# Layer 0 of a gated cross-attention kernel: transposes of two heads' probabilities in two 64-row halves of the TensorE array, with another order of the side work

## What is computed

```
x  = x + tanh(g_xattn[0]) * L0_xattn(layernorm(x), ctx, ctx)      # 16 heads of 16
x  = x + tanh(g_ffn[0])   * L0_ffn(layernorm(x))                  # scan over the sequences
...
scores = einsum('bhqd,bhkd->bhqk', qh, kh) * scale
attn   = softmax(scores)                                          # 112 x 375 for a head
out    = einsum('bhqk,bhkd->bhqd', attn, vh)
c      = sigmoid(..) * c + sigmoid(..) * tanh(..)                 # step of the scan, three gates
```

## Time and profile before

| | |
|---|---|
| median of 3 runs | 2946.25 us (2937.28 to 2954.1) |
| span of the profiled execution | 2561.4 us |
| around the span, against the median | 384.9 us |
| TensorE busy | 2366.4 us, 92% |
| VectorE, ScalarE, GpSimd busy | 66%, 60%, 28% |
| layer 0, first score to last exponential | about 38 to 790 us of the span |

### The profile page before, as it was taken

The page is one execution under the profiler, slowest core; times in us unless marked ns, Lnnn a source line. Parts: engine busy times, 40 slices in busy tenths (PEclk is TensorE's granted clock), DMA queues, the critical chain, the costliest instruction groups (busy, mean ns, idle before and its releaser), DMA issues. The chain is left out here.

```text
span 2561.4 us, 63498 instructions
## 1 busy us (share of the span) xinstructions
PE 2366.4 (92%) x20058; PEld 1795.7 (70%) x20059; DVE 1692.1 (66%) x5327; ACT 1525.4 (60%) x4611; POOL 729.2 (28%) x863
## 2 busy tenths in 40 slices
PE   7999999999998999999999999999999869999950
PEld 5777777777776566666666666666666658888840
DVE  4776776777674567767667767766776645555559
ACT  3777777777773656656666666665665425545530
POOL 2000000000000023322322332332332347777740
PEclk8999999999999999999999999999999989999975
DMA  5111111111113211111111111111110366666659
GB/s 155 44 36 48 46 36 48 45 42 42 45 35 95 72 30 47 42 35 41 42 40 37 42 44 32 47 42 30 47 42 28 110 211 187 186 186 188 188 186 380
DMA packets 145288, 210.06 MB, mean 82 GB/s; under 512 B 23976, under 2 KB 108506, under 8 KB 145026
## 3 DMA queue, kind: packets, MB, share of 16 engines
q1 hardware_dynamic: 114322, 139.92, 18.7%
q0 software_dynamic: 26544, 60.21, 7.0%
q10 hardware_dynamic: 4160, 6.55, 0.7%
HBM read 118.21 MB, written 96.75 MB: 84 GB/s over the span
## 5 line engine op out<-in xcount | busy, mean ns | idle before, releaser
L1454 ACT ACTIVATE wup<-bank,nmax 112x375 f32<-112x375 f32 x512 | 297.3, 585 | 127.2 <-DVE nmax L1558 126.0
L766 ACT ACTIVATE prob<-bank,nmax 112x375 f32<-112x375 f32 x512 | 293.6, 586 | 55.7 <-DVE nmax L850 51.6
L850 DVE TENSOR_REDUCE nmax<-bank 112x1 f32<-112x375 f32 x512 | 255.4, 541 | 90.2 <-PE bank L588 90.2
L2045 POOL DMA_INDIRECT expert_results<-res,dest x288 | 280.2, 973 | 118.5 <-ACT res L2163 67.0
L1558 DVE TENSOR_REDUCE nmax<-bank 112x1 f32<-112x375 f32 x512 | 255.4, 541 | 36.0 <-PE bank L1250 36.0
L1895 POOL DMA_INDIRECT expert_rows<-rows,ids x248 | 237.2, 957 | 78.6 <-issue 69.0
L2163 ACT ACTIVATE res<-bank,xr 128x256 f32<-128x256 f32 x288 | 136.4, 474 | 190.7 <-PE bank L2077 189.6
L1868 POOL TENSOR_TENSOR stats<-stats,neg_half 112x1 f32<-112x1 f32 x64 | 35.7, 557 | 654.6 <-DVE stats L1589 652.2
L1313 PE MATMUL bank<-wup,wk 128*128 128x375 f32 x512 | 219.8, 512 | 2.1 <-DMA wup<-context_turned 0.9
L1019 POOL TENSOR_TENSOR stats<-stats,neg_half 112x1 f32<-112x1 f32 x64 | 35.1, 549 | 633.7 <-DVE stats L880 629.7
L1460 ACT COPY pT<-bank 128x336 f32<-128x336 f32 x512 | 201.1, 449 | 19.7 <-PE bank L1257 19.1
(11 more groups left out here) (255 smaller groups left out, 5001.6 us busy)
## 6 DMA issues: line engine op xcount, KB each, us to landing
xr<-expert_rows SPq DMA_DIRECT2D x288, 129.0 KB
wup<-expert_results SPq DMA_DIRECT2D x14, 1024.0 KB, 18.8
wdn<-expert_results SPq DMA_DIRECT2D x14, 1024.0 KB, 20.2
wdn<-in_L_ffn_W_down_dram SPq DMA_DIRECT2D x8, 1024.0 KB, 12.2
expert_rows<-nowhere SPq DMA_DIRECT2D x56, 129.0 KB, 3.1
x_and_h_in<-stage SPq DMA_DIRECT2D x32, 224.0 KB, 2.6
xt<-x_and_h_in SPq DMA_DIRECT2D x32, 224.0 KB, 2.8
context_turned<-ctxT SPq DMA_DIRECT2D x32, 187.5 KB, 2.3
```

The source lines that it names most:

```text
L766: nc.scalar.activation(prob[:, n % RING, :NK], s_bank[r][:NQ, :NK], ACT.Exp, bias=nmax[:, r:r + 1], accum_out=rsum[:, par, h:h + 1]).then_ ...
L850: nc.vector.tensor_reduce(nmax[:, r:r + 1], s_bank[r][:NQ, :NK], AX, ALU.max, negate=True).then_inc(maxed, 1)
L1454: nc.scalar.activation(prob[:, n % RING, :NK], s_bank[r][:NQ, :NK], ACT.Exp, bias=nmax[:, r:r + 1], accum_out=rsum[:, par, n:n + 1]).then_ ...
L2045: nc.gpsimd.indirect_dma_start(results_d, bass.IndirectOffsetOnAxis(ap=dest[:, n % DEST:n % DEST + 1], axis=0), res[:, n % RES, :], None, ...
```

## The change

Two heads are now turned together (`turn_pair`), three chunks each, every chunk as two transposes: probability rows 0 to 63 into bank `pt_bank[0]`, rows 64 to 111 into `pt_bank[1]`, each in its own rows of the array. ScalarE copies the first bank (2 x 3 x 64 = 384 columns) and VectorE the second (2 x 3 x 48 = 288) for every pair; each pair waits until both copies of the pair before are done. TensorE's order is uses n, pair n, scores, pair n+2, uses n+1 to n+3. ORDER_A has other slots, r1 goes to VectorE's lane, and the reciprocals move to slots 5 and 12 of `parts`. The cut diff shows the list, then TensorE's, ScalarE's and VectorE's parts in that order; ScalarE's `inverse` serves r0 alone, and `keep_pair` is on each of the two engines one copy of the 64 or 48 columns of all six chunks of a pair.

```diff
 ORDER_A = [
-    (0, "pre", "ctxT", "dve"), (1, "post", "va1", "dve"), (2, "pre", "k0", "act"), (2, "post", "wo", "dve"),
-    (4, "pre", "k1", "act"), (4, "pre", "xT", "dve"), (5, "pre", "q", "act"), (5, "post", "lnT", "dve"),
-    (6, "post", "h_in", "act"), (7, "pre", "v2", "dve"), (8, "post", "gate_f", "act"), (9, "own", "r0", "act"),
-    (11, "post", "gate_g", "act"), (12, "own", "va0", "dve"), (13, "own", "r1", "act"), (15, "pre", "v01", "dve"),
-    (15, "post", "gate_i", "act"),
+    (0, "pre", "ctxT", "dve"), (1, "post", "va1", "dve"), (1, "pre", "k0", "act"), (2, "post", "wo", "dve"),
+    (3, "pre", "k1", "act"), (5, "pre", "xT", "dve"), (6, "pre", "q", "act"), (6, "post", "lnT", "dve"),
+    (7, "own", "r0", "act"), (9, "own", "va0", "dve"), (9, "post", "h_in", "act"), (10, "pre", "v2", "dve"),
+    (11, "post", "gate_f", "act"), (13, "post", "gate_g", "act"), (14, "pre", "v01", "dve"),
+    (15, "post", "gate_i", "act"), (15, "own", "r1", "dve"),
 ]
...
-                def turn(i, n):
-                    wait_kept(pe, i, n - 1)
-                    pe.wait_ge(exped, H * i + n + 1)
-                    for c in range(KC):
-                        mm = pe.transpose(pt_bank[n % 2][:, c * NQ:(c + 1) * NQ],
-                                          prob[:, n % RING, c * P:(c + 1) * P], ident[:NQ, :NQ])
+                def turn_pair(i, n):
+
+                    wait_kept(pe, i, n)
+                    pe.wait_ge(exped, H * i + n + 2)
+                    for a in range(2):
+                        for c in range(KC):
+                            at = a * KC + c
+                            for half, rows_of in enumerate((slice(0, HALF_Q), slice(HALF_Q, NQ))):
+                                width = rows_of.stop - rows_of.start
+                                mm = pe.transpose(pt_bank[half][:, at * width:(at + 1) * width],
+                                                  prob[rows_of, (n + a) % RING, c * P:(c + 1) * P], ident[rows_of, rows_of])
                     mm.then_inc(turned, 1)
...
-                        turn(i, n)
-                        turn(i, n + 1)
                         uses.run(hooks, i, n, par, first, last)
+                        turn_pair(i, n)
                         next_scores(i, par, g, last)
+                        turn_pair(i, n + 2)
                         uses.run(hooks, i, n + 1, par, first, last)
-                        turn(i, n + 2)
-                        turn(i, n + 3)
...
-                        keep_turned(i, n)
                         uses.run(hooks, i, n, par, first, last)
-                        keep_turned(i, n + 1)
+                        keep_pair(i, n)
+                        keep_pair(i, n + 2)
+                        next_exponentials(i, par, n, last)
                         uses.run(hooks, i, n + 1, par, first, last)
-                        next_exponentials(i, par, n, last)
-                        keep_turned(i, n + 2)
                         next_exponentials(i, par, n + 1, last)
...
+                def keep_inverse(v):
+                    def f(p, par, n):
+                        misc = full(dve, "dve", n)
+                        nc.vector.tensor_copy(rT[:, v, :], misc[:, :NQ]).then_inc(lane_free["dve"], 1)
+                    return f
...
-                    if n == 8:
+                    if n == 5:
                         inverse(i, par, 0)
-                    if n == 10:
+                    if n == 12:
                         inverse(i, par, 1)
...
                         parts(i, n, par, first, last)
+                        keep_pair(i, n)
                         next_maximum(i, par, n, last)
                         next_maximum(i, par, n + 1, last)
+                        keep_pair(i, n + 2)
+                        next_maximum(i, par, n + 2, last)
+                        next_maximum(i, par, n + 3, last)
                         uses.run(hooks, i, n + 1, par, first, last)
                         parts(i, n + 1, par, first, last)
-                        keep_turned(i, n + 3)
-                        next_maximum(i, par, n + 2, last)
-                        next_maximum(i, par, n + 3, last)
```

More of the change, by code:

```diff
@@ L440, in layer0_phase @@
     PT_RING = 16
-    DVE_KEEPS = (3, )
+    HALF_Q = P // 2
     def head(n):
@@ L448, in loads, with pairs @@
         return (j - par) * 8 + 16
[L450 to L460, removed]
+    def pairs(i, n):
+        return (H * i + n) // 2
     def place(name):
@@ L514, in wait_kept @@
         def wait_kept(eng, i, n):
-            by_dve, by_act = kept(i, n)
-            wait(eng, kept_dve, by_dve)
-            wait(eng, kept_act, by_act)
+            wait(eng, kept_dve, pairs(i, n))
+            wait(eng, kept_act, pairs(i, n))
         def freed(eng, j, name):
@@ L752, in full, with pT_pair @@
                 return lane_bank[lane]
+            def pT_pair(n):
+                return pT[:, n % PT_RING:n % PT_RING + 2, :].rearrange("p a (c q) -> p (a c) q", c=KC)
             def room_in_pT(eng, i, n):
@@ L764, in exponentials, with keep_pair @@
                         wait(act, inverted, NV * (i - 1))
-                    wait(act, turned, H * i + n + 1 - RING)
+                    if H * i + n >= RING:
+                        act.wait_ge(turned, pairs(i, n - RING) + 1)
                     nc.scalar.activation(prob[:, n % RING, :NK], s_bank[r][:NQ, :NK], ACT.Exp, bias=nmax[:, r:r + 1],
                                          accum_out=rsum[:, par, h:h + 1]).then_inc(exped, 1)
-                def keep_turned(i, n):
-                    act.wait_ge(turned, H * i + n + 1)
+                def keep_pair(i, n):
+                    act.wait_ge(turned, pairs(i, n) + 1)
                     room_in_pT(act, i, n)
-                    nc.scalar.copy(pT[:, n % PT_RING, :], pt_bank[n % 2][:, :KC * NQ]).then_inc(kept_act, 1)
+                    nc.scalar.copy(pT_pair(n)[:, :, 0:HALF_Q],
+                                   pt_bank[0][:, :2 * KC * HALF_Q].rearrange("p (a q) -> p a q", q=HALF_Q)).then_inc(kept_act, 1)
                 def q(j, par, n):
@@ L813, in _ @@
                 hooks = {"q": q, "k0": k(0), "k1": k(1), "gate_f": gate(0), "gate_i": gate(1), "gate_g": gate(2), "h_in": h_into,
-                         "r0": inverse(0), "r1": inverse(1)}
+                         "r0": inverse(0)}
                 uses.run(hooks, -1, None, 1, first=True)
@@ L850, in maximum, with keep_pair @@
                     nc.vector.tensor_reduce(nmax[:, r:r + 1], s_bank[r][:NQ, :NK], AX, ALU.max, negate=True).then_inc(maxed, 1)
-                def keep_turned(i, n):
-                    dve.wait_ge(turned, H * i + n + 1)
+                def keep_pair(i, n):
+                    dve.wait_ge(turned, pairs(i, n) + 1)
                     room_in_pT(dve, i, n)
-                    nc.vector.tensor_copy(pT[:, n % PT_RING, :], pt_bank[n % 2][:, :KC * NQ]).then_inc(kept_dve, 1)
+                    width = NQ - HALF_Q
+                    nc.vector.tensor_copy(pT_pair(n)[:, :, HALF_Q:NQ],
+                                          pt_bank[1][:, :2 * KC * width].rearrange("p (a q) -> p a q", q=width)).then_inc(kept_dve, 1)
+                def keep_inverse(v):
[3 more added lines that the diff above has]
+                    return f
                 def inverse(i, par, v):
@@ L950, in _ @@
                 hooks = {"xT": keep_xT, "ctxT": keep_ctxT, "wo": residual, "lnT": keep_lnT, "v01": keep_v((0, 1)), "v2": keep_v((2,)), "va0": normalise(0),
-                         "va1": normalise(1)}
+                         "va1": normalise(1), "r1": keep_inverse(1)}
                 nc.vector.memset(spare[:], 0.0).then_inc(spare_set, 1)
```

## The result

The changed kernel takes 3169.21 us (median of 4, 3163.81 to 3176.5) against 2941.77 us for the kernel before in the same comparison: 1.0772 times as long, with a 95% interval of 1.0747 to 1.0797. The forecast was 3083 us, slower by 137; it is slower by 227, beyond the top of the range (3140).

What follows compares the result with a forecast made beforehand. TensorE bounds layer 0 (97% busy): 22.3 us work plus 5.80 us stalls make 28.1 us a sequence against 23.67. Thirty sequences at 4.4, plus 4 and 1 for first and last, add 137 us: 3083 us, range 3030 to 3140.

Steps and rivals of the forecast that it cites:

- P at 0.51 us: TensorE's transposes of a pair of heads as concurrent halves: 0.51 us against 0.58 for 2 x 3 whole transposes.
- The rival with P at 0.82: Halves not side by side, or loading one after the other: pair 0.82 us, 1.4 us a sequence, 3128 us; chance 0.10.
- second P of group 0: TensorE's second pair in group 0 waits for VectorE's copy behind ctxT's copy and x's moments: stall 0.48 us.
- scores of group 2: TensorE's scores wait for all exponentials of group 1, with k0 ahead in ScalarE's queue: stall 0.37 us.
- second P of group 1: TensorE's second pair in group 1 waits for VectorE's copy, with norm_y ahead of it: stall 0.60 us.
- q: TensorE's q waits for xT, which VectorE copies behind four maxima and a second pair's copy: stall 1.74 us.
- r0: TensorE's r0, on ScalarE's bank, waits for q's evacuation, covered only by q and lnT: stall 1.51 us.
- gate_f: TensorE's gate_f waits for h_in's evacuation, with only a value block after h_in: stall 0.25 us.
- ctxT: TensorE's ctxT waits for r1's copy, as both use VectorE's bank: stall 0.53 us.
- scores of group 3: TensorE's scores wait for two exponentials that ScalarE has left behind q's evacuation: stall 0.32 us.
- the third rival: TensorE's clock falls to 1.2 GHz in half of the sequences, 1.5 us each: 24 us, 3107 us; chance 0.06.
- Around the span: Outside the profiled execution's 2561.4 us span: 384.9 us up to the median of 2946.25, added to the forecast span 2698.

Runs made afterwards that it cites:

- e_replan: Changed kernel with halves kept and slots and queue orders found anew by the calculated walk; 2936.94 us, 0.9990 of the kernel before.
- e_replan_whole: Changed kernel with slots and queue orders found anew for halves, but pairs turned whole by six whole-array transposes; 2952.78 us, 1.0039 of the kernel before.
- e_fill: Changed kernel with 14 idle transposes before q's wait for xT and 12 before r0's wait for q's evacuation; 3077.43 us, 1.0514 of the kernel before.
- e_before: The kernel before, unchanged, profiled again; time 2930.27 us, span 2928.5 us.
- e_fillq: Changed kernel with the 14 idle transposes in front of q alone, r0's stop left empty; 3123.53 us.
- e_fillr: Changed kernel with the 12 idle transposes in front of r0 alone, q's stop left empty; 3153.91 us.
- e_xT4: Changed kernel with xT at slot 4 instead of 5, so VectorE copies it before the four maxima; 3104.28 us, 1.0605 of the kernel before.
- e_keepfirst: Changed kernel with both stops filled by idle transposes and VectorE's copy of a group's first pair ahead of its parts; 3072.21 us, 1.0463 of the kernel before.

## Why the prediction was wrong

The direction held, and so did the mechanism as far as it was walked; the size did not. The step that failed is the term that the sum puts at nothing, a fall of TensorE's clock. By the prediction's own steps:

- **The halves.** P at 0.51 us: measured 0.51 (627.40 to 627.91). They run side by side, the loads too. TensorE's loads of that pair:

```profile
627.40 0.45 PEld L591 LDWEIGHTS bank<-ident,prob 64*128 64x128 f32 x12 [0.16 <-issue]
```

One such load lasts 0.14 us, the first two (64 rows and 48) both start within 0.01 us, and all twelve are through in 0.45: a step of 0.06 for two, as the sum had it. The rule of the Trainium skill, TensorEngine Tiling (Array Packing), section Key Properties, that tiles load and multiply in parallel, holds for these transposes too. The rival with P at 0.82 fell (its own terms make 0.81). The prediction's estimate by the Trainium skill, TensorE: Matmul & The Clock Gate, section LDWEIGHTS, was 0.107 us for a load of 128 columns. The trace disagrees: even two at a time six such steps would take 0.64 us, and six whole transposes with their loads pass in 0.58. In TensorE's work the halves gave back 0.56 us a sequence (e_replan against e_replan_whole), where the sum has 0.54.
- **The stalls.** From the trace after, with block lengths taken off, against the walk: second P of group 0 0.49 (0.48), scores of group 2 0.32 (0.37), second P of group 1 0.59 (0.60), q 1.80 (1.74), r0 1.51 (1.51), gate_f 0.19 (0.25), ctxT 0.53 (0.53). The scores of group 3 stalled 0.33 us (0.32) in e_fill and not in the changed kernel. None is off by over 0.07 us. In e_fill, where the clock stays up, the period is 28.32 (28.1) and layer 0 lasts 901 us, 147 more than in e_before, where the sum had 137: 7 us of the difference by the period, the rest in the first and last sequences, which I had put at 5 and which cost 7.
- **The clock: the step that failed.** I had seen that TensorE would stand still 3.8 of about 6 us, and made it the third rival, with a chance of 0.06, one sequence in two, and 1.5 us in each. The sum itself has nothing for it. It fell in every settled sequence and cost 2.40 us in each (30.72 - 28.32): 7.08 us at a mean of 0.56 behind a stretch with 2.23 of 5.22 us busy. Over 31 sequences that is 74 us; the layer's own difference is 977 - 901 = 76. What misled me was the earlier trace rows: a stretch busy 0.12 of 2.48 us came before a fall and one with 3.95 of 7.00 before none, and I took 2.2 of about 6 for nearer to the second, on one row each. And the price was a guess ("a part of the 22.3 at half speed"): the blocks from r0 to v2, 4.71 us at full clock, take 7.05. The 137 us of the sum and the 76 make 213 of the 227 measured; period and ends, as above, are 10 more.
- **The range.** Its top, 3140, allowed for a few drops of the clock beside another rival, not for one in each sequence. Either stop alone can bring the clock down, as e_fillq and e_fillr show, so a kernel with both was not the case of a few drops.
- **Around the span.** 384.9 us were no launch and end of the program but another course of layer 1 in the profiled execution. It did no harm, as it cancels in the difference; but the sign was there: no row accounts for them.
- **Hidden work.** That ScalarE's relief and VectorE's longer queue would be worth nothing but in the chains held: with the order mended (e_replan) TensorE is busy 98% and its two waits come to 10.3 us in 550.

## What to carry to other kernels

A step laid right ahead of its user costs what stands in the evacuating engine's queue between them: walk that queue instruction by instruction; here it was right to 0.1 us a stall for the order as planned, and it also found orders nearly without stalls (periods within 0.2 us). For edits of that order it was less good: the longer stop of r0 in e_xT4 and the new waits in e_keepfirst were not foreseen, so walk the queues again after each edit. Then ask of every stop that the walk finds what it does to TensorE's clock, and count a fall in every sequence as a case of its own: here one fall cost more (2.4 us) than the longest stall (1.8). And give each of two forms an order of its own before comparing them: halves won by 0.5% in one order, and between the best order found for each the whole pairs were not behind.

## What the runs showed of the hardware

- With one long stop a sequence, 1.35 to 2.1 us of printed idle time (e_fillq, e_fillr, e_xT4), the granted clock fell in every sequence or in every second. In the changed kernel, with two, most of 7 us in each then ran at the lower level, 1.2 GHz. Idle transposes in the stops, 14 and 12 of them, 1.7 and 1.5 us long, kept it at 1.00 and made the kernel 2.4% faster (3169 and 3077 us, each beside its own runs of before: 1.0772 and 1.0514 times).
- The same stop in the same work brought the clock down in one sequence and not in the next (e_fillq throughout, e_fillr up to 330 us).
- Loads of 64 and of 48 rows in two halves of the array run side by side: twelve, of 0.14 us each, in 0.45 us.
- A stop of 0.9 us a sequence at 97% busy, as in the kernel before, left it at 1.00 in the settled part.
- Where work at the lower level ran ahead of a stall it hid it: the scores of group 3 waited 0.33 us in e_fill and not at all in the slower kernel.
- VectorE's waits of 7 us a sequence in layer 1 have no releaser in the trace, and were in each timed kernel's profile but not in the first of the kernel before. What they are is open.
